# Value sum as three float32r passes, with the normalisation moved behind it, in a four-block graph network kernel

## The reference, cut to what matters

```python
for i in range(NUM_BLOCKS):                      # 4
    y = _cond_layer_norm(x, cond, s1_w[i], ...)
    # sparse attention, 4 heads of 128:
    q = (y @ wq + bq) * Dh ** (-0.5); k = y @ wk + bk; v = y @ wv + bv
    scores = einsum('ehd,ehd->eh', q[src], k[dst])
    ex = exp(scores - smax[src]); attn = ex / denom[src]
    x = x + segment_sum(attn * v[dst], src) @ wo + bo
    y = _cond_layer_norm(x, cond, s2_w[i], ...)
    x = x + relu(y @ m_w1[i] + m_b1[i]) @ m_w2[i] + m_b2[i]
```

## Time and profile before

| | |
|---|---|
| Median of 3 runs | 1874.02 us (1873.92 to 1874.54) |
| Profiled execution: its own time | 1876.6 us |
| Its span (first to last instruction) | 1874.8 us |
| PE busy | 1828.2 us, 98% |
| DVE busy | 1096.4 us, 58% |
| ACT busy | 754.6 us, 40% |
| POOL busy | 328.4 us, 18% |

### The profile page before, as it was taken

The page is one execution under the profiler, slowest core; times in us unless marked ns, Lnnn a source line. Parts: engine busy times, 40 slices in busy tenths (PEclk is TensorE's granted clock), DMA queues, the critical chain, the costliest instruction groups (busy, mean ns, idle before and its releaser), DMA issues.

```text
span 1874.8 us, 31740 instructions
## 1 busy us (share of the span) xinstructions
PE 1828.2 (98%) x11066; PEld 1523.5 (81%) x11066; DVE 1096.4 (58%) x2301; ACT 754.6 (40%) x1070; POOL 328.4 (18%) x393
## 2 busy tenths in 40 slices
PE   6999999999999999989999999899999999999998
PEld 6998454787888888878888888788888887888887
DVE  6998456535555667345555673455547834555485
ACT  4552211125565341245654412256544222556532
POOL 0000902300000633000004340000016400000173
PEclk9999999999999999999999999999999999999999
DMA  3003110211000110210001102101010112010011
GB/s 121 1 1 128 67 37 31 75 42 57 29 29 1 39 51 23 78 58 29 29 1 39 51 23 78 44 19 53 1 39 23 51 37 83 15 31 27 23 67 67
DMA packets 38738, 79.74 MB, mean 43 GB/s; under 512 B 10856, under 2 KB 10856, under 8 KB 38592
## 3 DMA queue, kind: packets, MB, share of 16 engines
q1 hardware_dynamic: 38592, 77.82, 12.4%
HBM read 66.14 MB, written 11.67 MB: 42 GB/s over the span
## 4 chain that ended last, share of the span: by engine, by line
PE 62%; issue 32%; DVE 2%; DVEq 1%; POOL 1%; DMA 1%; ACT 1%; SPq 0%; POOLq 0%; ACTq 0%
PE ps L1294 39%; PE ps L1319 5%; PE ps L1284 4%; PE ps L1352 4%; PE ps L1227 3%; PE ps L1345 2%; PE ps L1253 2%; PE ps L1358 2%; PE ps L1403 2%; DVE hot L863 1%; DMA x<-in_x_dram 1%; POOL film L536 0%; DVE hot L866 0%; DVEq L873 0%; DVEq L863 0%
## 5 line engine op out<-in xcount | busy, mean ns | idle before, releaser
L1319 PE MATMUL ps<-pT,v 128*128 128x256 f32 (+1 forms) x1600 | 370.2, 379 | 4.2 <-ACT pT L780 4.1
L719 ACT ACTIVATE s<-masked_s,small 128x1280 f32 (+1 forms) x156 | 213.2, 1367 | 338.6 <-DVE small L1000 338.6
L1294 PE MATMUL ps<-yT,w 128*128 128x512 f32 (+1 forms) x1728 | 330.1, 352 | 0.0
L1319 PEld LDWEIGHTS ps<-pT,v 128*128 128x128 f32 x1600 | 292.2, 190 | 42.9 <-ACT pT L780 11.8
L1294 PE MATMUL ps<-kh,q_parts 128*128 128x512 f32 (+3 forms) x1440 | 319.3, 366 | 6.3 <-DVE v L1082 3.4
L1294 PEld LDWEIGHTS ps<-yT,w 128*128 128x128 f32 x1728 | 280.6, 189 | 44.9
L1294 PEld LDWEIGHTS ps<-kh,q_parts 128*128 128x128 f32 (+1 forms) x1440 | 249.5, 190 | 54.1 <-issue 6.1
L1294 PE MATMUL ps<-w,kh 128*128 128x512 f32 (+1 forms) x960 | 235.3, 396 | 2.5 <-POOL kh L582 2.5
L780 ACT COPY pT<-ps 128x1408 f32<-128x1408 f32 (+1 forms) x160 | 206.9, 1293 | 3.8 <-PE ps L1407 3.8
L1294 PEld LDWEIGHTS ps<-w,kh 128*128 128x128 f32 (+1 forms) x960 | 174.3, 186 | 41.3 <-POOL kh L582 2.9
L997 DVE CUSTOM_DVE_ANT_0 masked_s<-ps,mask 128x1280 f32<-128x1280 f32 x96 | 143.2, 1492 | 90.3 <-PE ps L1294 90.3
(11 more groups left out here) (164 smaller groups left out, 1988.0 us busy)
## 6 DMA issues: line engine op xcount, KB each, us to landing
mask<-mask_dram SPq DMA_DIRECT2D x24, 640.0 KB, 4.1
w_raw<-in_L_gnn_m_w_dram SPq DMA_DIRECT2D x8, 1024.0 KB, 5.3
mask_y<-mask_dram SPq DMA_DIRECT2D x12, 640.0 KB, 3.9
mask_dram<-mask_out SPq DMA_DIRECT2D x10, 640.0 KB, 2.9
w_l<-in_L_gnn_W_dram SPq DMA_DIRECT2D x2, 2048.0 KB, 10.0
w_raw<-in_L_gnn_wq_dram SPq DMA_DIRECT2D x4, 1024.0 KB, 5.5
w_raw<-in_L_gnn_wk_dram SPq DMA_DIRECT2D x4, 1024.0 KB, 6.5
w_raw<-in_L_gnn_wv_dram SPq DMA_DIRECT2D x4, 1024.0 KB, 5.4
```

The source lines that it names most:

```text
L719: nc.scalar.activation(to, masked_of(u), ACT.Exp, bias=small[0:R, u % 2, 1:2], accum_out=small[0:R, u % 2, 2:3]).then_inc(exp_done, 1)
L1294: mine = mm(to, left(a), right(b), start=first and n == 0, stop=final and n == 2)
L1319: mine = mm(ps[:, 6 + gh % 2, 0:wd], v[:, t, h * P:(h + 1) * P], pT[:, gh % 2, t, 0:wd], start=(t == 0), stop=(t == NT - 1))
```

## The change

- The value sum becomes three float32r passes. ACT copies the transposed scores to `pT` rounded (the high part), in two halves of five node tiles; DVE makes the low part by subtraction (`weights_low`), also in two halves. V gets a high part (ACT) and a low part (DVE, `v_low_part`) in the V product.
- The low part of V has no room of its own. It lies in the place of the residual `x`, which SP therefore writes to DRAM ahead of V (`spill_x`) and reads back in the attention stage (tiles 0 and 1) and after it (tiles 2 to 9) (`reload_x`).
- The transposed reciprocal goes. POOL makes the reciprocals (`reciprocals`), SP writes them to DRAM with two DMAs per pair, waits for both, and reads them back spread over all partitions (`spread_reciprocals`). DVE only copies the value sum out of PSUM, and POOL multiplies it three pairs later (`scale_head_output`). POOL also takes the low part of the queries.
- ACT now copies the transposed scores of unit u before `exp(u + 1)`, where it had them after it. The first `split_head_outputs` of ACT come after the copies of the last unit, where they came before.
- The larger `pT` leaves four places for masks: `MASK_PLACE = (0, 1, 2, 3, 0, 2, 3, 0, 2, 3)`.

```diff
-MASK_PLACE = (0, 1, 2, 3, 4, 0, 2, 3, 4, 0)
+MASK_PLACE = (0, 1, 2, 3, 0, 2, 3, 0, 2, 3)
+HALVES = (range(0, NT // 2), range(NT // 2, NT))
...
+        v_low = at("x", 5120, "v_low", [P, NT, D], F32R)
+        v_sum = at("x", 5120, "v_sum", [P, NT, D])
...
+            def spread_reciprocals(gh, i):
+
+                sizes = [rows(2 * (gh // H) + k) for k in range(2)]
+                sp.wait_ge(rec_ready, i * U + 2 * gh + 2)
+                for k, R in enumerate(sizes):
+                    sp.dma_start(rec_dram[gh % 4, k * P:k * P + R].rearrange("(p o) -> p o", o=1),
+                                 rec[0:R, gh % 4, k:k + 1]).then_inc(rec_saved, 16)
+                sp.wait_ge(rec_saved, (i * GH + gh + 1) * 32)
+                wd = sum(sizes)
+                sp.dma_start(rep[:, gh % 4, 0:wd], rec_dram[gh % 4:gh % 4 + 1, 0:wd].broadcast_to([P, wd])).then_inc(rep_in, 16)
...
-                for t in range(2, NT):
-                    if t >= 5:
+                for t in range(2, 4):
+                    load_mask(t)
+                for gh in range(GH):
+                    spread_reciprocals(gh, i)
+                    if gh == 0:
+                        reload_x(0)
+                        reload_x(1)
+                    for t in range(4, NT):
                         old = max(n for n in range(t) if MASK_PLACE[n] == MASK_PLACE[t])
...
+                        last_use = UNITS.index((old // 2, H - 1, old % 2))
+                        if last_use // 2 == gh:
+                            sp.wait_ge(masked, i * U + last_use + 1)
+                            load_mask(t)
                 sp.wait_ge(turned, i * U + U)
                 load_w("M1", m_w1, i)
+                sp.wait_ge(head_out, i * GH + GH)
+                for t in range(2, NT):
+                    reload_x(t)
...
+            def reciprocals(gh, i):
+
+                g = gh // H
+                for k in range(2):
+                    R = rows(2 * g + k)
+                    pool.wait_ge(exp_done, i * U + 2 * gh + k + 1)
+                    pool.sem_inc(passed)
+                    nc.gpsimd.tensor_scalar(small[0:R, k, 3:4], small[0:R, k, 2:3], 0.5, None, ALU.max).then_inc(den_s, 1)
+                    pool.wait_ge(den_s, i * U + 2 * gh + k + 1)
+                    nc.gpsimd.tensor_tensor(rec[0:R, gh % 4, k:k + 1], small[0:R, k, 3:4], minus_one[0:R, :],
+                                            ALU.pow).then_inc(rec_ready, 1)
...
+            def pool_attention(i):
+
+                for gh in range(GH):
+                    reciprocals(gh, i)
+                    if gh + 2 < GH:
+                        q_part(gh + 2, i)
+                    if gh >= 3:
+                        scale_head_output(gh - 3, i)
+                scale_head_output(GH - 3, i)
...
@@ in ACT's exp(u, i)
-                if u >= 3:
-                    act.wait_ge(turned, i * U + u - 1)
+                if u >= 2:
+                    act.wait_ge(rec_ready, i * U + u - 1)
...
@@ in ACT's attention(c)
+                    R = rows(2 * g + k)
+                    act.wait_ge(turned, i * U + u + 1)
+                    for half in range(2):
+                        nc.scalar.copy(pT[:, 0, turned_places(gh, half), k * P:k * P + R], turn_bank(half, R)).then_inc(p_high, 1)
                     if u + 1 < U:
                         exp(u + 1, i)
                     if u == U - 1:
                         act.wait_ge(scored, i * U + U)
                         split_head_outputs(0, i)
                         split_head_outputs(1, i)
...
-                    act.wait_ge(turned, i * U + u + 1)
...
-                    nc.scalar.copy(pT[:, gh % 2, :, k * P:k * P + R], turn[:, :, 0:R]).then_inc(pT_out, 1)
...
@@ in DVE's attention(c)
                     if u + 1 < U:
                         mask(u + 1, i)
+                    if u == 0:
+                        v_low_part(NT - 1, i)
                     if k == 1 and u >= 2:
                         head_output(u // 2 - 1, i)
+                    weights_low(u, i)
...
@@ in PE's weigh(gh, part, i)
-                for t in range(5 * part, 5 * part + 5):
-                    mine = mm(ps[:, 6 + gh % 2, 0:wd], v[:, t, h * P:(h + 1) * P], pT[:, gh % 2, t, 0:wd],
-                              start=(t == 0), stop=(t == NT - 1))
+                place = turned_places(gh, part).start - HALVES[part][0]
+                for n, (a, b) in enumerate(((1, 0), (0, 0), (0, 1))):
+                    if b == 1:
+                        pe.wait_ge(p_ready, weights)
+                    for t in HALVES[part]:
+                        left = (v, v_low)[a][:, t, h * P:(h + 1) * P]
+                        mine = mm(sums(gh, wd), left, pT[:, b, place + t, 0:wd], start=(n == 0 and t == 0),
+                                  stop=(n == 2 and t == NT - 1))
```

More of the change, by code:

```diff
@@ L277, in masked_of, with turn_bank, sums, turned_places @@
         def masked_of(u):
-            return masked_s[0:rows(u % 2 + 2 * UNITS[u][0]), :] if u else s_first[:]
+            n = u % 2
+            return masked_s[0:rows(n + 2 * UNITS[u][0]), n, :] if u else s_first[:]
+        def turn_bank(half, R):
+            return ps_flat[:, (3 + 2 * half) * BANK:(3 + 2 * half) * BANK + NT // 2 * P].rearrange("p (t r) -> p t r", r=P)[:, :, 0:R]
+        def sums(gh, wd):
+            return ps[:, 7, gh % 2 * 2 * P:gh % 2 * 2 * P + wd]
+        def turned_places(gh, half):
+            first = HALVES[half][0]
+            return slice(first + half * (gh % 2) * (NT // 2), first + half * (gh % 2) * (NT // 2) + NT // 2)
         y = at("y", 0, "y", [P, 3, D])
@@ L440, in load_mask, with spill_x, reload_x @@
                 sp.dma_start(masks[MASK_PLACE[t]][:], mask_dram[t]).then_inc(mask_in[MASK_PLACE[t]], 16)
+            def spill_x(i):
+                for t in range(NT):
+                    sp.wait_ge(biased, i * 2 * NT + t + 1)
+                    sp.dma_start(x_spill[t * P:t * P + rows(t)], x[0:rows(t), t, :]).then_inc(x_spilled, 16)
+            def reload_x(t):
+                sp.dma_start(x[0:rows(t), t, :], x_spill[t * P:t * P + rows(t)]).then_inc(x_back[t], 16)
             def attention_loads(jl, c, i):
@@ L607, in pool_block @@
                             add_bias(t - 1, m2_qkv, c, 1)
+                    for gh in range(2):
+                        q_part(gh, i + 1)
+            for gh in range(2):
+                q_part(gh, 0)
             with pool.Fori(0, L - 1) as i:
@@ L993, in mask @@
                 dve.wait_ge(scored, i * U + u + 1)
-                if u >= 1:
-                    dve.wait_ge(exp_done, i * U + u)
+                if u >= 2:
+                    dve.wait_ge(turned, i * U + u - 1)
                 dve.sem_inc(passed)
@@ L1007, in head_output @@
                 dve.wait_ge(summed, i * GH + gh + 1)
[L1008 to L1010 removed]
+                nc.vector.tensor_copy(q[:, h, g * 2 * P:g * 2 * P + wd], sums(gh, wd)).then_inc(head_out, 1)
             def products(jl, c, norm):
@@ L1032, in products @@
                     if kind == "QP":
-                        q_part(a, c.block + 1)
                         continue
@@ L1093, in products @@
                         dve.wait_ge(biased, (2 * c.block + second) * NT + a + 1)
+                        if not second:
+                            dve.wait_ge(x_back[a], c.block * 16 + 16)
                         nc.vector.tensor_tensor(x[0:R, a, :], bank[0:R, :], x[0:R, a, :], ALU.add).then_inc(dve_out, 1)
```

152 lines of the change are left out of this document (88 added, 64 removed).

## The result

The changed kernel takes 2031.97 us (median of 4 runs, 2028.4 to 2032.57) against 1873.97 us before (median of 4, 1873.19 to 1874.54). The ratio is 1.0839, 95% interval 1.0821 to 1.0858: 158 us slower, where 17 us less were forecast. The profiled execution has a span of 2029.9 us.

What follows compares the result with a forecast made beforehand. PE was taken to set the pace in attention. Gains of 63 us over four blocks less 46 us of mask waits gave 17 us off, from 1874 to 1857 us; the range for eight in ten was 1834 to 1884.

Steps and rivals of the forecast that it cites:

- part 5: Masks in attention: reused places and SP's queue make DVE wait 4.1 us, three times a block, 46 us in all.
- rival (e): Reciprocal write in SP's queue: lands as late as its upper bound, 5.7 us; 1900 us, chance 0.03.
- Rival (b): PE's clock in attention falls during the new waits, 3.4 us each; twelve cost 41 us, 1898 us; five or more: chance 0.1.
- Part 1: Value sum on PE in attention: 15 float32r passes 0.12 us apart; PE's unit becomes 4.40 us, from 4.95.
- the rule weighed there: Trainium skill on PE: weight loads overlap matmuls only across row groups; a pass would be about 0.22 us.
- rival (d): PE's value sum: weight loads do not hide, 1.04 us more a unit, 2011 us; chance 0.02.
- Part 2: ACT and DVE in attention keep up with PE's 4.40 us unit without waits; 0.2 us of wait kept for the range.
- rival (c): DVE's chain in attention is longer than PE's, 4.6 us a unit: 23 us more, 1880 us; chance 0.1.
- 16.0 + 2.9 - 1.1 - 2.6: Attention, us a block: gains in units 3 to 31 and 32 to 38, losses at unit 39 and by WO subtractions.
- Part 3: Ends of the attention stage: start gains 2.3 us; WO starts 3.1 us after the last `turned`, losing 2.5 a block.
- Part 4: Spill and reload of `x` and V's split: hidden; without cover the reload would cost some 4 us a block.
- Sum without the mask waits: Whole kernel if masks arrive in time: 63 us off 1874, 1811 us; as a rival, chance 0.07.

Runs made afterwards that it cites:

- experiment 11: Changed kernel, read-back and the second of a pair's two reciprocal writes left out for all but the first four pairs of a block; 1977.78 us, ratio 1.054.
- experiment 1: Changed kernel without the reciprocals' write and read-back for all but the first four pairs of a block (wrong factors); 1814.19 us, ratio 0.9677.
- experiment 10: Changed kernel, read-back only for a block's first four pairs, the other pairs' reciprocals written 512 bytes apart in DRAM; 1859.64 us, ratio 0.9911.
- experiment 3: Changed kernel with mask loads issued ahead of the reciprocal writes in SP's queue; 1973.01 us, ratio 1.0524.
- experiment 6: Changed kernel with each read-back issued behind the next pair's writes, masks still behind both; 1960.82 us, ratio 1.0458.
- experiment 4: Changed kernel with masks ahead of the writes and each read-back a pair later, output complete; 1848.3 us, ratio 0.986.
- experiment 8: experiment 4 with reciprocals going through an SBUF row, each step a pair behind, and ACT's split ahead of its last copies; 1830.42 us, ratio 0.976.
- experiment 7: experiment 1 with ACT's split of the first two head-output tiles ahead of its last two copies; 1811.65 us, ratio 0.9662.
- experiment 9: experiment 8 with the last two pairs of a block saved and read back without the delay, whole output; 1811.31 us, ratio 0.9665.

## Why the prediction was wrong

**The step that failed is the landing of the small write in part 5.** It was taken as 2.1 us from the start of the second issue, bounded by 1.5 and 5.7. SP's wait alone was 7.4 us, with the issue 7.8, beyond the upper bound; where the view gives the landing it is 7.6 and 7.9 us (experiments 11 and 1). Both bounds came from loads of long rows, and the upper one from a load of 2 KB behind others. No row of before had elements of four bytes written side by side into DRAM, so no row bounded it from above, and 5.7 should not have been called a bound. The Trainium skill ("DMA: Bandwidth & Descriptors", Anatomy of one DMA) says that most of a DMA's fixed cost is the wait until the target confirms the last byte, and that this can be surprisingly long where the target is DRAM. The page says so of DMAs issued from GpSimd, as it does its 2.0 us; those here are issued from SP. The trace agrees: over a window from 903 to 917 us of the changed kernel, 0.35 us a digit, the DMA engines are busy from 907.2 to 910.7, with the read-back issued at 906.59 among it, and, but for one slice, idle until the wait ends at 916.27.

```profile
DMA  0000000000006895289152000000000000005000
```

With the landing as I took it, the forecast was nearly met: experiment 10's write waits 1.3 us, and its time is 1859.6, where 1857 was forecast. It is no full test, since 10 leaves out most read-backs, and the closeness is partly luck: its mask waits are 35 us, where 46 were forecast, and PE's work takes 15 us longer than in experiment 1 (1770.1 us busy against 1755.1), where nothing was forecast. Its mask waits of 2.9 us each, for 4.1, show that the layout of the chain in part 5, from `exp_done` over the write to the mask, was right in the main.

**A second slip stands behind it.** Even rival (e), the upper bound of 5.7, was priced as one delay per mask, 1900 us. I compared the landing with the slack of the mask and never SP's whole round (wait for the exponential, two issues, landing, read-back) with the pair of 8.8 us. From a wait of about 7.5 us on (8.82 less 0.84 for the writes, 0.32 for the read-back and the gaps) the round is longer than the pair, the delay adds up from pair to pair, and one mask is late by 12 to 21 us, not by 4. The mean wait, 7.4, is just short of that; but the waits differ, and the two issues, 0.8 us as a rule, take up to 2.9 where SP is behind, so that the rounds ahead of unit 17 come to 9.7 us and more. How much hangs on this can be estimated from the terms of part 5: with 7.8 us for 2.1 a mask wait is 9.8 us, all of them 115, and the time 1926. The other 106 us of the 2032 are this slip, the next one and the clock. Experiments 3 and 6 show the parts: mending the order alone takes the waits from 191 to 123 us, ending the backlog alone also to 123, both together to 27.

**A third: masks and read-backs were given the landings of a quiet kernel.** A mask lands in 3.9 us without the writes, 6.4 in the changed kernel and 11.0 in experiment 4. The Trainium skill ("DMA: Bandwidth & Descriptors", Queues, rings and completion order) says that a DMA engine's completion is signalled only after every earlier write of that engine has landed. By that alone a mask's signal would be late and its bytes not. The traces show the bytes late too. What the DMA engines moved, 0.4 us a number, around one mask of experiment 4 (from 933, issued at 934.88) and one of experiment 8 (from 929, issued at 930.88):

```profile
GB/s 0 0 0 1 1 0 90 100 110 90 61 61 72 0 90 51 38 38 13 38 38 38 38 38 38 64 26 192 371 309 160 74 64 13 41 0 0 0 0 0
...
GB/s 0 0 1 1 3 0 41 64 54 56 105 233 374 412 294 218 115 0 0 0 0 20 0 0 1 1 3 15 90 92 79 51 41 0 0 0 0 0 0 0
```

Behind the writes into DRAM the rate stays near 38 GB/s from 939.4 to 943 and has its peak 9.3 us after the issue; behind the writes into SBUF it has it 3.3 us after. The median landings are 11.0 and 5.1 us. So the writes hold up the transfer behind them and not only its signal; how, no run shows.

**Rival (b), the clock, came true as a consequence.** It was given a tenth, with falls of 6.8 us; the waits were three to five times as long as forecast, and the stretches at 0.50 reach 20.5 us, most of it idle. The work done at the lower clock cost some 27 us (2032 - 1814 - 191), and PE's busy time, 28 us longer than in experiment 1, says the same. In experiment 10, with waits of 3 us, 10 us are left beside the 35 us of waits (1859.6 - 1814.2 - 35.1). The mean granted clock there is 0.981, for 0.991 in experiment 1, so that they are at least in part the clock's; it is not in every wait that it falls (from 915 to 926 us, around a wait of 2.6 us, it is 1.00).

What held, by experiment 1. In its timeline stand the third `turned`, the last, and WO's first passes:

```profile
803.57 0.97 PE L1518 MATMUL ps<-ident,s 128*128 128x128 f32 x10
...
965.57 1.03 PE L1518 MATMUL ps<-ident,s 98*128 98x98 f32 x10 [1.07 <-ACT s L823]
...
969.50 4.52 PE L1401 MATMUL ps<-w,kh 128*128 128x512 f32 x12 [2.90 <-POOL kh L678]
```

- Part 1: 4.40 us a unit forecast, 4.41 measured. Weight loads hide under passes 0.12 us apart, so the rule weighed there (no overlap within a row group) does not hold here, and rival (d) falls.
- Part 2: DVE keeps up; rival (c) falls. Third to last `turned` takes 162.1 us (966.60 - 804.54) against 179.5 before: 17.5 us a block, where 16.0 + 2.9 - 1.1 - 2.6 = 15.2 were forecast. The subtractions of WO cost about 0.4 us a block (two units of 4.62 and 4.61 us), not 2.6. The start of the stage, from the scores at 807.36 in the earlier trace rows to the third `turned`, took 16.4 us and takes 14.5 (790.00 to 804.54): a gain of 1.9, where 2.3 were forecast.
- Part 3: WO starts 2.9 us after the last `turned` (3.1 forecast). What I missed is that its first twelve passes then take 4.5 us, 3.0 before: a window from 969.5 to 972.6 us (below) has the clock at 0.50, behind a wait of only 2.9 us. The sum of 3.1 us had ACT's copies and split ahead of POOL's part; with ACT's split out of the way (experiment 7) 2.3 us remain, behind POOL's scaling of the last outputs.
- Part 4: spill and reload are hidden: experiment 9 has both, and DMA is 1% of its chain.
- Sum without the mask waits: 1811 forecast, 1814 measured (experiment 1), and 1811 with the whole output (experiment 9). The closeness comes in part from errors that cancel: the middle of the stage gained 2.3 us a block more than forecast, and WO's slow start took 1.5 that were not in the sum.

The window behind WO's first wait in experiment 1, columns as in the earlier trace rows:

```profile
969.50:972.60 3.10, 3.10 (x7) 2.48 (x8) 0.00 (x0) 1.28 (x3) 2.23 (x2) 0.50 0.64 240
```

## What to carry to other kernels

Don't write a column of SBUF into DRAM as four-byte neighbours: put it into a row of SBUF first, or at least 64 bytes apart (tried here only without reading it back), and let nothing that is urgent travel behind such writes. Where one queue waits for its own DMAs in a loop, compare its whole round with the period of the loop before pricing a single delay; above the period the delay grows with each turn. When no row shows a kind of transfer, the upper bound is missing, and the range must say so, or the transfer be measured first.

## What the hardware showed unexpectedly

- 256 elements of four bytes from 128 partitions: SP waited 7.2 to 8.6 us side by side in DRAM, 1.3 us at 64 or 512 bytes apart, 1.5 us into one row of SBUF; 128 elements side by side were waited for 7.7 us, 256 for 7.6.
- Such writes slow other transfers: a mask of 640 KB landed in 11.0 us when issued behind them (median of 24), in 3.9 without them, in 5.1 behind writes into SBUF; its bytes moved late, not only its signal.
- Around PE's waits of some 21 and 13 us the clock was 0.50 for 20.5 and 13.7 us, from within the wait into work that had begun again: nine score passes took 3.57 us, elsewhere 1.98.
